# A fixed order of work on five engines, planned with other costs and other due times

## The chip, the cores and the metric

One core of one Trainium2 chip. The metric is the device time of one launch in microseconds, lower is better.

## What is computed

A "macaron" block on x of shape 4 x 2048 x 256, float32: half an MLP, attention, half an MLP, each on a layer-normalised input and added to x.

```
x = x + 0.5 * ffn(layernorm(x))
x = x + attention(layernorm(x))
x = x + 0.5 * ffn(layernorm(x))
```

`ffn` is a gated MLP of width 704, in which the input of each product and each weight is first rounded to a 4-bit grid in blocks of 16 (`scale = max|x|/6`, then the nearest of 0, 0.5, 1, 1.5, 2, 3, 4, 6). `attention` is causal differential attention: 8 heads, each with two score maps of head dimension 16 over queries and keys that are rms-normalised and rotated; the output of a head is `softmax1 @ v - lam * softmax2 @ v`, layer-normalised, then projected.

## The kernel before

The 8192 rows are 64 tiles of 128 rows, and four tiles are a chunk: 16 chunks, 4 to each of the 4 batches. A chunk passes through six kinds of work. (1) First MLP: `stats` and `rstd` (layer norm), then for each pair of tiles `quant_x`, `divide_x`, `square_x`, `grid_x`, `points_x`, `dequant_x`, `high_x`, `low_x` (the 4-bit rounding, split into two float16 halves) and `turn_x`, a transposing DMA; for each tile three `hidden` products (L1311), `tanh` and `gate` for each, the same chain of rounding for the hidden row (`quant_h` ... `turn_h`), the `down` product (L1324), and `add_down`. (2) Projections: `norm_x`, `transpose_x` (L1300), `copy_xT`, `project_qk` and `project_v` (L1332), `read_qk`, `read_v`, `rope`, `rope_add`. (3) `rms` for the chunk, then `norm_qk`, `high_qk`, `low_qk`, `turn_qk` for each tile. (4) Attention of the chunk: for each of 4 groups of two heads and each key tile up to the diagonal one step. A step has two `scores` stages (L1347), two `exp` stages (L1074), a `mask` on the diagonal, and one `values` stage (L1365). A chunk has 16, 32, 48 or 64 steps by its place in its batch, 640 in all. Each group ends in `copy_o`, `transpose_o` (L1372), `heads_out`. (5) `head_stats`, `norm_heads`, `transpose_x`, `project_out` (L1379), `add_out`. (6) Second MLP, as the first, and the store.

PE (tensor) has all products and transposes; DVE (vector) the statistics, scales, gates, the low halves and sums; ACT (scalar) tanh, squares, copies and exp; POOL (gpsimd) four of the rounding steps, `rope_add`, `low_qk`, `mask` and `rstd`; SP issues the DMAs. `rms` (L1214) and `head_stats` (L1270) are one row and then the helper `rsqrt` (L465 to L474), twelve small DVE instructions that wait for one another.

What sets the order: `whole_plan` lists every stage with its engine, its weight (us), a due time, what it needs, which buffers it takes and which it frees. `Plan.order` then places stages one at a time. Among the stages whose needs are met it takes the one that can start first, and of those that can start at once the one with the smallest due time. The result is one list for each engine, and the emission below walks through these lists. So each engine's queue is fixed when the kernel is built, and a stage that waits holds back all behind it on its engine. The rings of buffers (two score buffers, three of probabilities, three shared PSUM banks, the MLP's rows and others) are dealt out in the order in which the plan takes them, and the waits for a free buffer follow from that.

The weights come from `COST`, or from `whole_plan` for `scores`, `exp` and `values`. To those of every engine but PE `START` (0.05) is added, and between engines `LAG` (0.12) passes. The due times come from `DUE`: `lead` and `spans` lay out the chunks on an axis (`spans` by the chunk's place in its batch), the pairs `mlp1`, `qkv`, `qk`, `out`, `mlp2` are an offset and a pace in hundredths of the chunk's span, and `nudge` shifts each kind of stage by a number of its own.

Of the kernel before, what the change touches and what calls it, by code (L numbers as in the profile page):

```python
# [44 lines left out]
NTC = 4  # L45
# [10 lines left out]
DUE = dict(lead=57, spans=(23, 55, 57, 15), tail=50208, early=1.97, mlp1=(85, 27), qkv=(-162, 60), qk=(-77, 71), out=(-188, 149), mlp2=(99, 30),  # L56
           nudge=dict(add_down=-22, add_out=18, copy_o=13, copy_xT=50, dequant_h=-57, dequant_x=-38,
                      divide_h=38, divide_x=5, down=-15, exp=222, gate=-22, grid_h=8, grid_x=-8,
                      head_stats=27, heads_out=29, hidden=-47, high_h=-47, high_qk=-154, high_x=15,
                      load=6, low_h=-29, low_qk=3, low_x=28, mask=-58, norm_heads=-50, norm_qk=-4,  # L60
                      norm_x=-27, points_x=31, project_out=-16, project_qk=-9, quant_h=61,
                      quant_x=57, read_qk=-26, read_v=-15, rms=2, rope=19, rope_add=30, rstd=40,
                      scores=-242, square_h=-29, stats=-37, store=-29, tanh=32, transpose_o=-26,
                      transpose_x=-28, turn_h=6, turn_qk=5, turn_x=-26, values=5))
# [16 lines left out]
COST = dict(add_down=0.46, add_out=0.42, copy_o=0.68, copy_xT=0.38, dequant_h=1.42, dequant_x=1.12,  # L81
            divide_h=1.45, divide_x=1.11, down=2.19, gate=0.82, grid_h=1.72, grid_x=1.33, head_stats=4.21,
            heads_out=3.64, hidden=1.27, high_h=0.79, high_qk=1.14, high_x=0.63, low_h=1.18, low_qk=2.46,
            low_x=1.03, mask=0.69, norm_heads=0.55, norm_qk=0.87, norm_x=0.6, points_h=1.71, points_x=1.29,
            project_out=1.09, project_qk=2.13, project_v=1.0, quant_h=1.83, quant_x=2.78, read_qk=0.6,
            read_v=0.38, rms=7.63, rope=1.93, rope_add=1.38, rstd=2.9, square_h=1.61, square_x=1.29,
            stats=2.3, tanh=0.46, transpose_o=0.58, transpose_x=0.33)
START = 0.05
LAG = 0.12


def attention_steps():


    out, diagonals = [], 0
# [17 lines left out]
class Plan:  # L113
# [12 lines left out]
    def add(self, name, engine, weight, due, needs=(), takes=(), frees=(), lands=0.0):  # L126
        weight = COST.get(name[0], weight)
# [3 lines left out]
    def order(self):  # L131
        end, free_at = {}, dict.fromkeys(ENGINES, 0.0)
# [1281 lines left out]
```

## Time and profile before

| | |
|---|---|
| median of 3 runs | 2468.85 us (2467.5 to 2469.09) |
| the profiled execution | 2471.45 us |
| its span, first to last instruction | 2469.5 us |
| mean granted clock of TensorE | 0.937 |

The rows of the trace are given below, in groups. A busy time is that of an engine's own instructions; waiting at a semaphore is idle. PE is the matrix engine, PEld its weight loads, which overlap it.

### The profile page before, as it was taken

The page shows a single profiled execution, that of the slowest core. Times are in us where ns is not written, and L with a number is a line of the kernel's source. Part 1 is how long each engine was busy: PE and PEld are TensorE (multiplying, and loading weights), DVE is VectorE, ACT ScalarE, POOL GpSimd, SP SyncE. Part 2 cuts the span into 40 slices and gives each one's busy share as a digit, 9 for nine tenths or more (in the row PEclk, how much of TensorE's full clock was granted, in tenths as well). Part 3 has the DMA queues.
Part 4 walks back from the last instruction along what each step waited for, and adds up shares of the span by engine and source line. Part 5 has one row for each costly group of instructions (what it writes and reads, how often), then busy time and mean ns, then how long its engine had stood idle before and what let it go on. Part 6 is the DMA issues. An engine that isn't in the chain of part 4 may idle for free.

```text
span 2469.5 us, 39323 instructions
## 1 busy us (share of the span) xinstructions
PE 2099.7 (85%) x13502; PEld 839.6 (34%) x13502; DVE 1831.3 (74%) x3615; ACT 1777.8 (72%) x2660; POOL 1658.3 (67%) x1520
## 2 busy tenths in 40 slices
PE   1567999899897889899998889989898889998965
PEld 1233433233333333333333333333333333332322
DVE  6888787668758888777858888886867888873434
ACT  2345677978875778778786778877787677887852
POOL 3887666766756687876766677886776677862415
PEclk8788999999998999999998999999999999998986
DMA  3122322221312132232321322223241223221101
GB/s 92 34 40 55 65 49 49 47 53 30 68 39 52 19 63 50 56 66 44 55 58 19 53 48 63 60 33 71 33 84 21 47 32 79 49 50 34 33 1 41
DMA packets 409906, 119.36 MB, mean 48 GB/s; under 512 B 390638, under 2 KB 409454, under 8 KB 409710
## 3 DMA queue, kind: packets, MB, share of 16 engines
q1 hardware_dynamic: 409710, 116.86, 25.1%
q8 instruction: 109, 1.79, 0.3%
q14 instruction: 87, 0.71, 0.1%
HBM read 11.96 MB, written 8.39 MB: 8 GB/s over the span
## 4 chain that ended last, share of the span: by engine, by line
PE 45%; DVE 20%; ACT 8%; POOL 5%; issue 5%; DMA 2%; SPq 1%; ACTq 0%; DVEq 0%; POOLq 0%
PE psum_o L1365 11%; PE shared L1311 10%; PE shared L1324 7%; PE psum_s L1347 7%; ACT probs L1074 6%; PE shared L1332 4%; PE shared L1379 3%; DVE nwt L473 2%; DVE nwt L472 2%; DVE h L1166 1%; PE shared L1300 1%; DMA q_stack<-st_q 1%; DVE nwt L474 1%; POOL grid L965 1%; POOL hq L961 1%
## 5 line engine op out<-in xcount | busy, mean ns | idle before, releaser
L1074 ACT ACTIVATE probs<-psum_s 128x1024 f32<-128x1024 f32 (+3 forms) x1280 | 1092.0, 896 | 234.2 <-PE psum_s L1347 170.9
L1365 PE MATMUL psum_o<-probs,v_sb 128*32 128x512 f32 (+3 forms) x5120 | 590.6, 546 | 9.5 <-POOL probs L995 8.9
L1311 PE MATMUL shared<-w_gu_T,xT 128*128 128x480 f16 (+1 forms) x2304 | 522.6, 371 | 68.5 <-DMA xT<-x 44.4
L1347 PE MATMUL psum_s<-q_stack,k_stack 64*128 64x512 f16 (+3 forms) x2560 | 431.7, 359 | 113.6 <-ACT probs L1074 97.1
L1324 PE MATMUL shared<-w_down_T,hT 128*128 128x256 f16 (+1 forms) x2176 | 315.5, 292 | 77.3 <-DVE hq L1156 55.9
L1347 PEld LDWEIGHTS psum_s<-q_stack,k_stack 64*128 64x128 f16 x2560 | 110.1, 93 | 652.6 <-ACT probs L1074 465.9
L1311 PEld LDWEIGHTS shared<-w_gu_T,xT 128*128 128x128 f16 x2304 | 207.1, 99 | 352.7 <-issue 119.4
L995 POOL TENSOR_SCALAR_AFFINE_SELECT probs<-probs 128x512 f32<-128x512 f32 x256 | 172.6, 679 | 225.7 <-ACT probs L1074 224.4
L961 POOL TENSOR_TENSOR hq<-grid,hq 128x704 f32<-128x704 f32 x128 | 222.7, 1740 | 99.8 <-ACT grid L1019 99.7
L1009 ACT ACTIVATE hq<-shared,tanh_scale 128x240 f32<-128x240 f32 (+1 forms) x384 | 172.6, 454 | 155.7 <-PE shared L1311 143.9
L1324 PEld LDWEIGHTS shared<-w_down_T,hT 128*128 128x128 f16 (+1 forms) x2176 | 204.1, 103 | 193.5 <-issue 76.6
L1154 DVE SCALAR_TENSOR_TENSOR hq<-hq,shared 128x240 f32<-128x240 f32 (+1 forms) x384 | 147.6, 384 | 131.2 <-ACT hq L1009 130.1
L937 POOL TENSOR_TENSOR hq<-hq,rscale 128x704 f32<-128x704 f32 x128 | 186.9, 1463 | 80.0 <-DVE rscale L1100 80.0
L965 POOL TENSOR_TENSOR grid<-hq,grid 128x704 f32<-128x704 f32 x128 | 224.8, 1756 | 8.5
L1166 DVE TENSOR_TENSOR h<-hq,h 128x704 f16<-128x704 f32 x128 | 157.7, 1232 | 63.7 <-ACT h L1027 63.2
L1332 PE MATMUL shared<-w_qkv_T,xT 128*128 128x512 f32 (+1 forms) x512 | 196.9, 517 | 1.3 <-ACT xT L1036 0.8
L969 POOL TENSOR_TENSOR hq<-grid,qscale 128x704 f32<-128x704 f32 x128 | 182.7, 1427 | 8.9
L1365 PEld LDWEIGHTS psum_o<-probs,v_sb 128*32 128x32 f32 x5120 | 110.5, 109 | 186.0 <-issue 145.6
L1156 DVE SCALAR_TENSOR_TENSOR hq<-hq,shared 128x240 f32<-128x240 f32 (+1 forms) x384 | 152.8, 398 | 13.2
L1019 ACT ACTIVATE grid<-grid 128x704 f32<-128x704 f32 (+1 forms) x192 | 141.5, 737 | 6.1
L986 POOL TENSOR_TENSOR st_q<-roped,st_q 128x512 f16<-128x512 f32 x64 | 79.0, 1235 | 90.7 <-ACT st_q L1064 90.6
L1027 ACT ACTIVATE h<-hq 128x704 f16<-128x704 f32 x128 | 100.8, 788 | 42.1 <-POOL hq L969 28.7
(120 smaller groups left out, 2848.2 us busy)
## 6 DMA issues: line engine op xcount, KB each, us to landing
xb<-L_attn_x SPq DMA_DIRECT2D x16, 512.0 KB, 4.0
out<-xb SPq DMA_DIRECT2D x16, 512.0 KB, 3.3
hT<-h SPq DMA_TRANSPOSE x128, 3.5
xT<-x SPq DMA_TRANSPOSE x64, 3.1
k_stack<-st_k SPq DMA_TRANSPOSE x64, 3.3
q_stack<-st_q SPq DMA_TRANSPOSE x64, 3.3
k_stack<-L_ffn_w_down SPq DMA_DIRECT2D x1, 704.0 KB, 8.7
k_stack<-L_ffn_w_gate SPq DMA_DIRECT2D x1, 480.0 KB, 4.6
```

The source lines that it names most:

```text
L937: nc.gpsimd.tensor_tensor(by_block(a), by_block(a), rscale[:, i, 0:nb].unsqueeze(2).broadcast_to([P, nb, QB]), ALU.mult).then_inc(scaled_r ...
L961: nc.gpsimd.tensor_tensor(a, g, a, ALU.add).then_inc(grid_ready, 1)
L965: nc.gpsimd.tensor_tensor(g, a, g, ALU.subtract).then_inc(grid_ready, 1)
L969: nc.gpsimd.tensor_tensor(by_block(a), by_block(g), qscale[:, i, 0:nb].unsqueeze(2).broadcast_to([P, nb, QB]), ALU.mult).then_inc(quantise ...
L995: nc.gpsimd.affine_select(out=blk, in_=blk, compare_op=ALU.is_ge, fill=0.0, base=0, pattern=[[0, 4], [1, P]], channel_multiplier=-1)\
L1074: nc.scalar.activation(probs[:, s % 3, 2 * u:2 * u + 2, q0:CHUNK], psum_s[u][:, :, q0:CHUNK], ACT.Exp, scale=HD ** -0.5 / QK_SCALE ** 2).t ...
L1166: nc.vector.tensor_tensor(low, buffers(kind, key)[0], high, ALU.subtract)\
L1311: last = nc.tensor.matmul(bank(e)[:, 0:2 * (hi - lo)], xs[:, x, t % 2, k, :], w_gu_T[:, w, k, 2 * lo:2 * hi], start=n == 0, stop=n == len( ...
L1324: last = nc.tensor.matmul(bank(e)[:, 0:C], hs[0:n, k, :], w_down_T[0:n, w, :], start=i == 0, stop=i == len(parts) - 1)
L1332: last = nc.tensor.matmul(bank(e)[:, 0:hi - lo], xT[:, XT[1, t] % ROWS, k, :], w_qkv_T[:, k, lo:hi], start=k == 0, stop=k == KC - 1)
L1347: last = nc.tensor.matmul(psum_s[u][:, j, q0:CHUNK], k_stack[half, at, h, kt % NTC * P:(kt % NTC + 1) * P], q_stack[half, c % 2, h, q0:CHU ...
L1365: last = nc.tensor.matmul(psum_o[at:at + VD, q0:CHUNK], v_sb[:, kt // NTC % SLOTS * NTC + kt % NTC, 2 * g + u, :], probs[:, s % 3, 2 * u + ...
```

## The change

Every instruction stays, and the code that emits them is untouched. The plan changes in these points.

- `START` and `LAG` go. A stage now leaves its engine `OVERLAP` earlier than its weight says (0.08 DVE, 0.10 ACT, 0.04 POOL), while its result is ready only at the full weight, on PE 0.14 later (`DRAIN`). A stage of another engine meets it after `REACH` (0.04 to 0.14 by the engine that waits), a freed buffer after `RELEASE` (0.06).
- PE's tiling is followed: `scores` and `values` each have one of their own and all else a third. A PE stage whose tiling is another than the last one's starts `SWITCH` (0.11) later, and the choice of the next stage sees that.
- The costs are new; those of `rms` and `head_stats` rise, those of `project_qk`, `project_v` and `values` fall.
- `norm_x` of a chunk from the fourth on needs the last `norm_heads` of the chunk three before.
- `DUE` is wholly new.

```diff
--- before.py
+++ after.py
@@ -53,15 +53,15 @@
 
 
 
-DUE = dict(lead=57, spans=(23, 55, 57, 15), tail=50208, early=1.97, mlp1=(85, 27), qkv=(-162, 60), qk=(-77, 71), out=(-188, 149), mlp2=(99, 30),
-           nudge=dict(add_down=-22, add_out=18, copy_o=13, copy_xT=50, dequant_h=-57, dequant_x=-38,
-                      divide_h=38, divide_x=5, down=-15, exp=222, gate=-22, grid_h=8, grid_x=-8,
-                      head_stats=27, heads_out=29, hidden=-47, high_h=-47, high_qk=-154, high_x=15,
-                      load=6, low_h=-29, low_qk=3, low_x=28, mask=-58, norm_heads=-50, norm_qk=-4,
-                      norm_x=-27, points_x=31, project_out=-16, project_qk=-9, quant_h=61,
-                      quant_x=57, read_qk=-26, read_v=-15, rms=2, rope=19, rope_add=30, rstd=40,
-                      scores=-242, square_h=-29, stats=-37, store=-29, tanh=32, transpose_o=-26,
-                      transpose_x=-28, turn_h=6, turn_qk=5, turn_x=-26, values=5))
+DUE = dict(lead=6900543696, spans=(22, 77, 47, 13564), tail=3021347, early=0.16, mlp1=(9, 17), qkv=(-59, 98), qk=(-183, 113), out=(-142, 85), mlp2=(207, 79),
+           nudge=dict(add_out=-7, copy_o=-67, copy_xT=-18, dequant_h=5, dequant_x=-1, divide_x=-28,
+                      down=15, exp=-12, gate=43, grid_h=6, grid_x=4, head_stats=102, heads_out=-15,
+                      hidden=89, high_h=-4, high_qk=211, high_x=-3, load=11, low_h=4, low_qk=-30,
+                      low_x=79, mask=14, norm_qk=-4, norm_x=-8, points_h=-131, points_x=-11,
+                      project_out=-20, project_qk=10, project_v=120, quant_h=-5, quant_x=-17,
+                      read_qk=54, read_v=34, rms=30, rope=110, rope_add=63, rstd=57, scores=-167,
+                      square_h=-5, square_x=28, stats=101, store=-7, tanh=-107, transpose_o=-7,
+                      transpose_x=-11, turn_h=20, turn_qk=-6, values=34))
 ST = 2
 LANDING = 4.0
 XU = 2
@@ -78,15 +78,19 @@
 HALF = P // 2
 
 KTILES = [(lo + i * (hi - lo) // 2, (hi - lo) // 2) for lo, hi in PARTS for i in range(2)]
-COST = dict(add_down=0.46, add_out=0.42, copy_o=0.68, copy_xT=0.38, dequant_h=1.42, dequant_x=1.12,
-            divide_h=1.45, divide_x=1.11, down=2.19, gate=0.82, grid_h=1.72, grid_x=1.33, head_stats=4.21,
-            heads_out=3.64, hidden=1.27, high_h=0.79, high_qk=1.14, high_x=0.63, low_h=1.18, low_qk=2.46,
-            low_x=1.03, mask=0.69, norm_heads=0.55, norm_qk=0.87, norm_x=0.6, points_h=1.71, points_x=1.29,
-            project_out=1.09, project_qk=2.13, project_v=1.0, quant_h=1.83, quant_x=2.78, read_qk=0.6,
-            read_v=0.38, rms=7.63, rope=1.93, rope_add=1.38, rstd=2.9, square_h=1.61, square_x=1.29,
-            stats=2.3, tanh=0.46, transpose_o=0.58, transpose_x=0.33)
-START = 0.05
-LAG = 0.12
+COST = dict(add_down=0.47, add_out=0.42, copy_o=0.68, copy_xT=0.38, dequant_h=1.43, dequant_x=1.1,
+            divide_h=1.46, divide_x=1.1, down=2.07, gate=0.82, grid_h=1.74, grid_x=1.37, head_stats=6.25,
+            heads_out=3.38, hidden=1.23, high_h=0.79, high_qk=1.14, high_x=0.63, low_h=1.23, low_qk=2.48,
+            low_x=0.96, mask=0.68, norm_heads=0.45, norm_qk=0.88, norm_x=0.82, points_h=1.76, points_x=1.37,
+            project_out=0.87, project_qk=1.75, project_v=0.87, quant_h=2.05, quant_x=2.87, read_qk=0.59,
+            read_v=0.37, rms=9.04, rope=1.93, rope_add=1.32, rstd=2.7, square_h=1.61, square_x=1.29,
+            stats=1.81, tanh=0.45, transpose_o=0.56, transpose_x=0.28)
+OVERLAP = dict(tensor=0.0, vector=0.08, scalar=0.1, gpsimd=0.04, sync=0.0)
+REACH = dict(tensor=0.14, vector=0.04, scalar=0.04, gpsimd=0.08, sync=0.1)
+RELEASE = 0.06
+DRAIN = 0.14
+TILING = dict(scores=1, values=2)
+SWITCH = 0.11
 
 
 def attention_steps():
@@ -125,7 +129,9 @@
 
     def add(self, name, engine, weight, due, needs=(), takes=(), frees=(), lands=0.0):
         weight = COST.get(name[0], weight)
-        self.stages[name] = (engine, weight + START * (engine != "tensor"), due + self.nudge.get(name[0], 0),
+        if engine == "tensor":
+            lands += DRAIN
+        self.stages[name] = (engine, weight, due + self.nudge.get(name[0], 0),
                              [n for n in needs if n], list(takes), list(frees), lands)
 
     def order(self):
@@ -134,6 +140,7 @@
         self.ring = {r: {} for r in self.sizes}
         banks = [[0.0, 0] for _ in range(BANKS)]
         out = {e: [] for e in ENGINES}
+        tiling, left = 0, {}
         missing = {name: len(stage[3]) for name, stage in self.stages.items()}
         needed_by = {name: [] for name in self.stages}
         for name, stage in self.stages.items():
@@ -169,6 +176,8 @@
                 at = ready(name)
                 if at is not None:
                     start = max(at, free_at[self.stages[name][0]])
+                    if self.stages[name][0] == "tensor" and TILING.get(name[0], 0) != tiling:
+                        start += SWITCH
                     if best is None or (round(start, 6), place[name]) < best[:2]:
                         best = (round(start, 6), place[name], start, name)
             assert best, "stages that wait for one another: " + str(list(met)[:20])
@@ -182,18 +191,20 @@
                     banks[b] = [math.inf, banks[b][1] + 1]
                 else:
                     self.ring[r].setdefault(user, len(self.ring[r]))
-            free_at[engine] = start + weight
+            free_at[engine] = left[name] = start + weight - OVERLAP[engine]
+            if engine == "tensor":
+                tiling = TILING.get(name[0], 0)
             end[name] = start + weight + lands
             for n in needed_by[name]:
                 missing[n] -= 1
                 if not missing[n]:
-                    met[n] = max(end[m] + (LAG if self.stages[m][0] != self.stages[n][0] else 0)
-                                 for m in self.stages[n][3])
+                    met[n] = max(end[m] + REACH[self.stages[n][0]] if self.stages[m][0] != self.stages[n][0] else
+                                 left[m] for m in self.stages[n][3])
             for r, user in frees:
                 if r == "bank":
-                    banks[self.bank[user][0]][0] = end[name] + LAG
+                    banks[self.bank[user][0]][0] = end[name] + REACH["tensor"]
                 else:
-                    freed[r][self.ring[r][user]] = end[name] + LAG
+                    freed[r][self.ring[r][user]] = end[name] + RELEASE
             out[engine].append(name)
         self.length = max(end.values())
         self.end = end
@@ -301,7 +312,8 @@
         roots(("stats", 1, c), s0 + (due["qkv"][0] - 2) * k, [("add_down", 0, t) for t in tiles])
         for i, t in enumerate(tiles):
             d = s0 + (due["qkv"][0] + due["qkv"][1] * i) * k
-            add(("norm_x", 1, t), "vector", .5, d, [("rstd", 1, c)], [("xrow", (1, t))],
+            add(("norm_x", 1, t), "vector", .5, d,
+                [("rstd", 1, c), ("norm_heads", NTC * (c - 2) - 1) if c >= 3 else None], [("xrow", (1, t))],
                 [("stats", (1, c))] if i == NTC - 1 else [])
             transposed(1, t, d + .5, [("norm_x", 1, t)])
             before = lambda name: (name, t - 1) if t else None
@@ -334,15 +346,15 @@
             w = (CHUNK - q0) / CHUNK
             for u in range(2):
                 before = s - 1 + u, 1 - u
-                add(("scores", s, u), "tensor", .24 * w, d + u * .1,
+                add(("scores", s, u), "tensor", .22 * w, d + u * .1,
                     [("turn_qk", tiles[-1]), ("scores", s - 1, 1) if s else None],
                     [("scores", (s, u))])
-                add(("exp", s, u), "scalar", .12 + .85 * w, d + u * .1,
+                add(("exp", s, u), "scalar", .17 + .855 * w, d + u * .1,
                     [("scores", s, u), ("exp", *before) if s or u else None], [("probs", s)], [("scores", (s, u))])
             if diag is not None:
                 add(("mask", s), "gpsimd", .62, d + .3, [("exp", s, 1)])
             d += (CHUNK - q0) * k
-            add(("values", s), "tensor", .94 * w, d, [("mask", s) if diag is not None else ("exp", s, 1),
+            add(("values", s), "tensor", .87 * w, d, [("mask", s) if diag is not None else ("exp", s, 1),
                                                       ("values", s - 1) if s else None, ("read_v", tiles[-1])],
                 [("psum_o", (c, g))], [("probs", s)])
             if is_last:
```

## Rows read from the trace of the kernel before

**Rows 1.** The page's span and busy time of each engine
```profile
span 2469.5 us, 39323 instructions
...
PE 2099.7 (85%) x13502; PEld 839.6 (34%) x13502; DVE 1831.3 (74%) x3615; ACT 1777.8 (72%) x2660; POOL 1658.3 (67%) x1520
```

**Rows 2.** Windows, whole core; columns us, busy us, granted clock, DMA share, GB/s
```profile
0.00:80.00 80.00, 14.53 (x71) 11.75 (x72) 54.19 (x118) 21.79 (x44) 36.62 (x49) 0.80 0.30 77
80.00:300.00 220.00, 164.88 (x920) 77.45 (x918) 183.32 (x336) 116.74 (x202) 171.72 (x140) 0.85 0.29 52
300.00:2200.00 1900.00, 1721.57 (x11239) 680.84 (x11241) 1483.64 (x2934) 1469.81 (x2193) 1347.88 (x1241) 0.96 0.26 49
2200.00:2390.00 190.00, 158.93 (x1117) 48.62 (x1115) 74.74 (x161) 149.95 (x190) 64.93 (x62) 0.94 0.15 30
2390.00:2469.50 79.50, 39.79 (x164) 20.91 (x164) 35.39 (x72) 19.55 (x34) 37.18 (x30) 0.67 0.15 32
```

**Rows 3.** Windows of 100 us, the same columns
```profile
700.00:800.00 100.00, 85.71 (x558) 34.54 (x555) 75.89 (x155) 68.90 (x110) 59.99 (x63) 0.91 0.19 36
...
1300.00:1400.00 100.00, 84.16 (x588) 36.55 (x584) 81.11 (x162) 66.77 (x110) 59.68 (x60) 0.93 0.22 36
...
1900.00:2000.00 100.00, 83.73 (x569) 35.24 (x568) 83.36 (x183) 67.91 (x108) 61.61 (x73) 0.91 0.22 38
2100.00:2200.00 100.00, 97.32 (x633) 39.76 (x635) 79.72 (x154) 80.80 (x121) 79.61 (x67) 1.00 0.23 46
```

**Rows 4.** Waits of PE, 300 to 2200; us in total, times, longest us
```profile
PE psum_s L1347 <- ACT probs L1074: 79.1, 161, 1.6
PE shared L1324 <- DVE hq L1156: 31.2, 9, 5.3
PE shared L1300 <- DVE hq L1156: 19.1, 4, 6.8
PE shared L1300 <- DVE xb L1173: 9.1, 4, 2.4
...
PE shared L1300 <- DVE xrow L1277: 5.7, 4, 2.3
PE shared L1311 <- DVE hq L1156: 5.4, 3, 4.9
```

**Rows 5.** Groups of instructions, busy us, mean ns, idle before: rms and head_stats
```profile
L473 DVE TENSOR_TENSOR nwt<-nwt 128x32 f32<-128x32 f32 (+1 forms) x96 | 51.3, 535 | 3.3
L472 DVE TENSOR_TENSOR nwt<-nwt 128x32 f32<-128x32 f32 (+1 forms) x96 | 50.1, 522 | 3.3
...
L474 DVE SCALAR_TENSOR_TENSOR nwt<-nwt 128x128 f32<-128x128 f32 (+1 forms) x64 | 37.4, 584 | 2.2
...
L465 DVE TENSOR_SCALAR nwt<-nwt 128x128 f32<-128x128 f32 (+1 forms) x32 | 25.1, 785 | 1.1
...
L466 DVE TENSOR_SCALAR nwt<-nwt 128x128 uint32<-128x128 uint32 (+1 forms) x32 | 19.7, 617 | 0.0
L468 DVE TENSOR_SCALAR nwt<-nwt 128x128 int32<-128x128 int32 (+1 forms) x32 | 18.9, 591 | 1.1
...
L1270 DVE TENSOR_SCALAR nwt<-head_ssq 128x32 f32<-128x32 f32 x16 | 11.9, 746 | 0.4
...
L1214 DVE TENSOR_SCALAR nwt<-qk_ssq 128x128 f32<-128x128 f32 x16 | 11.2, 698 | 0.4
```

**Rows 6.** Source line L466; ns min/median/max, first and last start us
```profile
L466 DVE TENSOR_SCALAR nwt<-nwt x32: 168/217/1724, 174.6 to 2387.1; 128x128 uint32<-128x128 uint32 x16, 128x32 uint32<-128x32 uint32 x16
```

**Rows 7.** Timeline of ACT from 807, of PE from 704; start us, us
```profile
807.61 7.56 ACT L1074 ACTIVATE probs<-psum_s 128x1024 f32<-128x1024 f32 x8
...
704.32 0.60 PE L1347 MATMUL psum_s<-q_stack,k_stack 64*128 64x512 f16 x4
704.86 1.06 PE L1365 MATMUL psum_o<-probs,v_sb 128*32 128x512 f32 x8
705.89 0.39 PE L1347 MATMUL psum_s<-q_stack,k_stack 64*128 64x512 f16 x2
```

## The prediction

> **What bounds the kernel now.** I read the page's first part first: TensorE is busy 2099.7 of 2469.5 us, the other three engines 67 to 74% [rows 1]. PE's own work is the largest sum. As the change keeps every instruction, time can come only from the 370 us in which PE stands still, or from the clock at which it works. The profiled execution took 2471.45 us, 1.95 around its span; that is 2.6 above the median of the runs, 2468.85. The sum below is made against 2471.45.
>
> The stretches say where PE stands still [rows 2]. The first 80 us prepare the weights (65 us idle, nothing of it planned by this code). From 80 to 300 the first chunks fill the machine (55 idle). From 300 to 2200 all passes run beside one another: 1721.57 of 1900 busy, 178.4 idle, mean granted clock 0.96. From 2200 to 2390 the last attention chunk runs with little beside it (31 idle), and the last 79.5 us are the last chunk's output and second MLP, with nothing left beside them (40 idle). The long middle is where an order can matter. Its hundreds of microseconds are not alike [rows 3]: 2100 to 2200 has 97.3 us of PE at full clock, while 700, 1300 and 1900 have 84 to 86 at 0.91 to 0.93. These three lie where one batch ends and the next begins with its short causal chunks.
>
> Who ended PE's waits in the middle [rows 4]: exp freeing a score buffer, 79.1 us in 161 short waits of 0.5 us; and long waits at the head of the queue, the `down` products and the transposes L1300 behind DVE work, 31.2 us in 9 waits (3.5 each) and 19.1 in 4 (4.8 each), with 20.2 in 11 more on the next three rows. The first kind belongs to the two-deep score ring. The second is what a wrong plan looks like: PE's fixed list puts an item next whose input or bank is several microseconds late, and all the attention queued behind it stands too. DVE rows end 70.5 us of these.
>
> **The change part by part.** No instruction is added or removed, in compute or in DMA; each engine's list, SP's included, is permuted, and buffers are dealt again to users. So the price of a part is only what it does to waits.
>
> *DVE costs and overlap.* The list of DVE must be in step with the others. Two stages, `rms` and `head_stats`, are a scalar row and the inverse-root helper, 16 calls each. Their eight main rows add up to 25.1+19.7+18.9+50.1+51.3+37.4+11.9+11.2 = 225.6 us, 7.05 us per call [rows 5]. The old plan held them for (7.63+4.21)/2+0.05 = 5.97, the new one for (9.04+6.25)/2-0.08 = 7.57. So the old lists were 1.08 us late at each of 32 calls, 35 us in all; the middle is 1900 of the 2212 us in which these calls occur [rows 6], so 30 us of it. DVE is busy 78% there [rows 2], and I let its free 22% absorb that share: 23 us reaches PE, as part of the 70.5 us above. The bounds are 0 and 70.5 less, and on the other side nothing excludes a loss: the boundary windows bound it, below. I take 23 because it is the one lateness that rows measure.
>
> *ACT and PE costs.* Eight full exps back to back take 7.56 us, 0.945 each [rows 7]; the old plan says 1.02, the new one 0.925. On PE two full scores stages take 0.54 (704.32 to 704.86) and the values stage up to the next scores 1.03 (704.86 to 705.89) [rows 7]. The old plan has 2 x 0.24 and 0.94, no switch; the new one 2 x 0.22+0.11 and 0.87+0.11. So the old plan saw an attention step as 2.04 of ACT against 1.42 of PE, where the rows give 1.89 against 1.57 and the new plan 1.85 against 1.53. It believed that there was 0.6 us of room for MLP work per step, and there was 0.3. Correcting that can thin out the 79.1 us of exp waits, or add to them, if more exps are set in a row with nothing between. Ends: 79 less; or, if the middle waited at the last attention stretch's rate (31 of 190 idle against 178 of 1900), (31/190-178.4/1900) x 1900 = 132 more. I take 0, since the ring's depth stays and these waits are short.
>
> *`norm_x` needs the `norm_heads` of three chunks before* (c from 3, 13 chunks, 52 stages). Both are DVE's, so no wait is emitted, only the order is tied. Projection runs ahead of output by design; cost 0, unless it is what holds a batch's first projections back (rival 3).
>
> *Reach, release, drain.* A uniform 0.12 becomes 0.04 to 0.14 by engine, 0.14 after PE. These decide near-ties among items that start within a tenth of a microsecond. 0 of itself; ends included in the two above.
>
> *The new due times* set which of several ready stages goes first. Head and tail: from 80 to 300 and after 2390 the chain of dependencies has few alternatives; I take 0 for both, with ends of 20 less (under half of the 55 idle) and 15 more.
>
> *Clock.* In the middle the granted clock is 0.96, the mix of the two levels 2.4 and 1.2 GHz, so 1900 x 0.04 = 76 us of full clock are missing. The windows where PE is best filled have 1.00, the worst 0.91 [rows 3]. If waits shrink by 23 of 178, a like part of 76 is 10 us; half of it, 5, since part of the slow time is PE waiting anyway. Ends 0 and 20.
>
> Sum: 2471.45 - 23 - 5 = 2443.
>
> **The rivals.** *1. Much faster.* All of the misplaced items go, and the middle runs at 95% of PE, between its mean 90.6 and its best window. 1721.57/0.95 = 1812, 88 less: 2383. For it: such windows exist in this very trace [rows 3]. Against: two thirds of the 178 us then have to go, with the exp waits left in place.
>
> *2. No change.* A fixed list can hold only a mean, and the real durations are not near theirs. L466, one small DVE operation, takes 168 ns at least, 217 at the median and 1724 at most [rows 6], mean 617 [rows 5]. So (617-217)/617 = 65% of its time is standing. If the eight rows stand alike, 0.65 x 225.6 = 146 us is standing; a fifth more, 29 us, in an order that packs DVE and POOL closer gives all 28 us back: 2470. POOL, the engine that a closer packing sets beside it, is busy 71% of the middle [rows 2].
> The Trainium skill (GPSIMD Engine Reference, Specifications and Key points) says that GpSimd shares its SBUF interfaces with VectorE and contends with DVE instructions that use two ports or have two SBUF inputs. This would be the cause of that spread, and speaks against a plan that gains by closer packing; the trace shows the spread in L466 but names no cause. By that rule the sum is this rival's, by the mean costs alone it is the forecast's.
>
> *3. Slower: the batch boundary.* The due positions of the projections are parts of the chunk's own span, and the new spans are 22, 77, 47 and 13564. For the first chunk of batches 2 to 4 the span is the long one. With qkv=(-59, 98) its four tiles are due at -59, 39, 137 and 235% of it; its scores, from 100% on. So where several are ready, tiles 2 and 3 lose against the batch's other work, although no score of that chunk can start before all four are turned. In the old plan, (-162, 60) puts all four before 18%. Attention would then be missing at the three boundaries, where PE is already weak: 14.3+15.8+16.3 = 46.4 us idle in three windows [rows 3]. Doubling that: 2471.45 + 46.4 - 28 = 2490. It decides from the point at which the boundaries lose more than 28 us, 9 each. Against: a ready projection on an idle PE is taken whatever its due time, since the earliest start goes first, and norm and transposes precede it by needs alone.
>
> **How the numbers follow.** About 0.2% is what a measurement of this kernel can tell from no change, some 5 us. Forecast 0.56, rival 1 0.11, rival 2 0.13, rival 3 0.20. Faster 0.67, same 0.13, slower 0.20. The forecast's own range, with the clock, head and a part of the exp term, is 2410 to 2463. The whole range reaches to rival 1 (2385) and into rival 3 as far as 2482, with about 0.08 left out below and 0.11 above.
>
> **What would show it.** Right: instruction counts alike; in the middle PE's long waits behind DVE (L1324, L1300, L1311) fall from 70 us to under 50, their longest from 5 to 7 us to 3 or 4; PE busy about alike or slightly smaller, clock above 0.96; the middle about 28 us shorter, head and tail within 10. Exp waits near 79 us. The two DVE stages near 7 us per call. Wrong: waits behind DVE alike or larger; exp waits over 110; a dip below 80 at each batch boundary with scores waiting for the q_stack transfer (rival 3); the mean of L466 and its kin up by a fifth and DVE's busy sum up by 25 us or more (rival 2); or a gain that lies in the first 300 or last 270 us.

## The result, and the profile of the changed kernel

The changed kernel takes 2477.45 us (median of 20 runs, 2467.07 to 2484.6), the kernel before 2469.28 on the same chips: ratio 1.0031, 95% interval 1.0022 to 1.004. It is slower by 0.31%, some 8 us. The forecast was 2443. The rows below are from an execution of 2476.07 us. Lines 465 to 474 of before are 477 to 486 now, as all later lines 12 higher.

The page of the changed kernel, span and busy time of each engine:

```profile
span 2474.1 us, 39316 instructions
...
PE 2060.2 (83%) x13502; PEld 844.6 (34%) x13502; DVE 1854.0 (75%) x3615; ACT 1773.8 (72%) x2660; POOL 1670.0 (67%) x1520
```

Against [rows 1] the counts are the same, PE is busy 39.5 us less, DVE 22.7 us more. So PE does the same work in less time, and stands idle 413.9 us where it was 369.8, 44.1 more. That is the whole riddle: the change gave PE 39.5 us and took 44.1 away. The granted clock, 0.942 against 0.937, is the higher of the two and has no part in the loss.

Its windows, in the columns of [rows 2]; the first three are the hundreds of microseconds in which batches meet, the last four whole stretches:

```profile
700.00:800.00 100.00, 85.11 (x579) 34.50 (x583) 75.27 (x154) 73.24 (x113) 63.39 (x65) 0.91 0.21 38
1300.00:1400.00 100.00, 84.12 (x591) 37.97 (x589) 88.21 (x177) 68.75 (x114) 66.68 (x68) 0.91 0.22 39
1900.00:2000.00 100.00, 86.24 (x608) 37.12 (x604) 90.78 (x192) 70.85 (x115) 65.20 (x74) 0.91 0.23 38
...
80.00:300.00 220.00, 160.43 (x865) 80.80 (x864) 194.54 (x337) 112.33 (x200) 185.35 (x148) 0.88 0.29 53
300.00:2200.00 1900.00, 1685.58 (x11223) 680.61 (x11222) 1495.99 (x2927) 1462.61 (x2182) 1344.56 (x1230) 0.96 0.26 49
2200.00:2390.00 190.00, 160.72 (x1187) 50.32 (x1185) 70.72 (x149) 158.02 (x203) 66.90 (x65) 0.98 0.17 32
2390.00:2474.10 84.10, 39.58 (x164) 21.07 (x164) 39.60 (x89) 19.66 (x34) 37.21 (x30) 0.66 0.14 30
```

The boundary windows are as weak as before and no weaker [rows 3], and the middle does about the same number of products in 1900 us (11223 against 11239) with 36 us less of PE's busy time [rows 2].

Waits of PE from 300 to 2200 us in the changed kernel; us in total, times, longest us:

```profile
PE psum_s L1359 <- ACT probs L1086: 113.5, 224, 1.7
PE psum_o L1377 <- DVE o_sb L1245: 15.4, 11, 2.6
PE shared L1336 <- DVE hq L1168: 10.3, 6, 2.1
PE shared L1323 <- DVE hq L1168: 10.1, 11, 1.9
PE shared L1312 <- DVE hq L1168: 9.8, 11, 2.4
...
PE shared L1312 <- DVE xrow L1289: 7.1, 8, 1.6
PE shared L1323 <- DVE xb L1185: 4.3, 6, 1.2
```

The long waits that I had read as the plan's error are gone. Those of L1336, L1312 and L1323 behind DVE add up to 47.4 us in eight rows (five of them above, three small) and the longest is 2.4 us, not 6.8. In [rows 4] they were 70.5, and 72.2 with one small row that it leaves out. But other waits have come behind DVE: all of them together are 71.0 us, 74.6 before, in 73 short ones instead of 31. Over the whole span they are 131.8 us, 130.7 before. And exp now ends 113.5 us of PE's waits, 34.4 more than in [rows 4].

Groups of instructions of the changed kernel; busy us, mean ns, idle before:

```profile
L485 DVE TENSOR_TENSOR nwt<-nwt 128x32 f32<-128x32 f32 (+1 forms) x96 | 48.5, 505 | 3.3
...
L478 DVE TENSOR_SCALAR nwt<-nwt 128x128 uint32<-128x128 uint32 (+1 forms) x32 | 20.7, 647 | 0.0
...
L1145 DVE TENSOR_SCALAR xq<-xb,mean_var,rstd 128x256 f32<-128x256 f32 x128 | 116.5, 950 | 14.3 <-POOL rstd L969 14.0
...
L1178 DVE TENSOR_TENSOR h<-hq,h 128x704 f16<-128x704 f32 x128 | 173.4, 1355 | 54.7 <-ACT h L1039 54.5
...
L1289 DVE TENSOR_TENSOR xrow<-heads,head_rstd 128x256 f32<-128x256 f32 x64 | 40.3, 666 | 9.0 <-PE shared L1312 8.5
```

The same three groups in the trace of before, which stand in no row ahead of the prediction:

```profile
L1166 DVE TENSOR_TENSOR h<-hq,h 128x704 f16<-128x704 f32 x128 | 157.7, 1232 | 63.7 <-ACT h L1027 63.2
L1133 DVE TENSOR_SCALAR xq<-xb,mean_var,rstd 128x256 f32<-128x256 f32 x128 | 83.6, 694 | 9.2 <-POOL rstd L957 9.0
L1277 DVE TENSOR_TENSOR xrow<-heads,head_rstd 128x256 f32<-128x256 f32 x64 | 27.0, 453 | 6.8 <-PE shared L1300 6.2
```

This is where the plan's picture breaks. The same instructions on the same data have other durations in another order. The two stages of [rows 5] fell from 225.6 to 194.2 us (their eight rows, 6.07 us a call; the new plan holds 7.57 for them), while L1145 rose by 32.9, L1178 by 15.7 and L1289 by 13.3. The new costs of `rms` (9.04), `head_stats` (6.25) and `quant_x` (2.87) are their mean durations in the old trace, from first to last instruction. They describe the order that the plan has just thrown away.

### The profile page after: what moved, and what is told of

The parts are those of the page before. It is cut to its first block, busy times and chain, and to the rows that moved or that the text cites. A ratio compares the mean times of both kernels' runs of the same rounds, so it can differ in the third digit from the quotient of the medians.

```text
span 2474.1 us, 39316 instructions
## 1 busy us (share of the span) xinstructions
PE 2060.2 (83%) x13502; PEld 844.6 (34%) x13502; DVE 1854.0 (75%) x3615; ACT 1773.8 (72%) x2660; POOL 1670.0 (67%) x1520
## 4 chain that ended last, share of the span: by engine, by line
PE 31%; DVE 29%; ACT 12%; POOL 10%; issue 7%; DMA 3%; SPq 1%; ACTq 0%; DVEq 0%; POOLq 0%
PE psum_o L1377 9%; ACT probs L1086 9%; PE shared L1336 5%; PE shared L1323 5%; PE psum_s L1359 4%; PE shared L1344 4%; DVE amax L1109 3%; DVE xq L1145 2%; DVE h L1178 2%; POOL grid L977 2%; PE shared L1391 2%; DVE hq L1168 2%; DVE qscale L1111 2%; POOL hq L973 2%; POOL hq L949 2%
## 5 line engine op out<-in xcount | busy, mean ns | idle before, releaser
L1086 ACT ACTIVATE probs<-psum_s 128x1024 f32<-128x1024 f32 (+3 forms) x1280 | 1067.9, 898 | 180.7 <-PE psum_s L1359 154.5
L1377 PE MATMUL psum_o<-probs,v_sb 128*32 128x512 f32 (+3 forms) x5120 | 608.4, 566 | 37.1 <-DVE o_sb L1245 16.2
L1323 PE MATMUL shared<-w_gu_T,xT 128*128 128x480 f16 (+1 forms) x2304 | 495.1, 366 | 65.9 <-DMA xT<-x 44.5
L1359 PE MATMUL psum_s<-q_stack,k_stack 64*128 64x512 f16 (+3 forms) x2560 | 407.2, 360 | 149.0 <-ACT probs L1086 136.0
L1336 PE MATMUL shared<-w_down_T,hT 128*128 128x256 f16 (+1 forms) x2176 | 302.2, 284 | 58.5 <-DVE hq L1168 41.1
L1323 PEld LDWEIGHTS shared<-w_gu_T,xT 128*128 128x128 f16 x2304 | 218.0, 99 | 326.8 <-issue 62.4
L1359 PEld LDWEIGHTS psum_s<-q_stack,k_stack 64*128 64x128 f16 x2560 | 98.9, 94 | 588.4 <-ACT probs L1086 497.8
L1336 PEld LDWEIGHTS shared<-w_down_T,hT 128*128 128x128 f16 (+1 forms) x2176 | 201.2, 100 | 176.6 <-issue 77.0
L1166 DVE SCALAR_TENSOR_TENSOR hq<-hq,shared 128x240 f32<-128x240 f32 (+1 forms) x384 | 147.8, 385 | 103.5 <-ACT hq L1021 102.8
L1178 DVE TENSOR_TENSOR h<-hq,h 128x704 f16<-128x704 f32 x128 | 173.4, 1355 | 54.7 <-ACT h L1039 54.5
L1377 PEld LDWEIGHTS psum_o<-probs,v_sb 128*32 128x32 f32 x5120 | 116.3, 111 | 272.3 <-issue 193.6
L1344 PE MATMUL shared<-w_qkv_T,xT 128*128 128x256 f32 (+1 forms) x512 | 191.8, 509 | 16.2 <-DVE hq L1168 10.5
L1029 ACT ACTIVATE grid<-hq 128x704 f32<-128x704 f32 x128 | 101.5, 793 | 49.9 <-POOL hq L949 49.8
```

Source lines behind the costliest of these rows:

```text
L1086: nc.scalar.activation(probs[:, s % 3, 2 * u:2 * u + 2, q0:CHUNK], psum_s[u][:, :, q0:CHUNK], ACT.Exp, scale=HD ** -0.5 / QK_SCALE ** 2).t ...
L1178: nc.vector.tensor_tensor(low, buffers(kind, key)[0], high, ALU.subtract)\
L1323: last = nc.tensor.matmul(bank(e)[:, 0:2 * (hi - lo)], xs[:, x, t % 2, k, :], w_gu_T[:, w, k, 2 * lo:2 * hi], start=n == 0, stop=n == len( ...
L1336: last = nc.tensor.matmul(bank(e)[:, 0:C], hs[0:n, k, :], w_down_T[0:n, w, :], start=i == 0, stop=i == len(parts) - 1)
L1344: last = nc.tensor.matmul(bank(e)[:, 0:hi - lo], xT[:, XT[1, t] % ROWS, k, :], w_qkv_T[:, k, lo:hi], start=k == 0, stop=k == KC - 1)
L1359: last = nc.tensor.matmul(psum_s[u][:, j, q0:CHUNK], k_stack[half, at, h, kt % NTC * P:(kt % NTC + 1) * P], q_stack[half, c % 2, h, q0:CHU ...
```

## The experiments

**What makes a duration depend on the order.** The timelines of DVE and of POOL in the kernel before, side by side in the same microseconds, suggest it; start us, us:

```profile
808.48 0.42 DVE L1259 TENSOR_REDUCE head_ssq<-o_norm 128x8 f32<-128x256 f32 x1
808.93 1.52 DVE L1270 TENSOR_SCALAR nwt<-head_ssq 128x32 f32<-128x32 f32 x1
810.49 0.18 DVE L465 TENSOR_SCALAR nwt<-nwt 128x32 f32<-128x32 f32 x1
810.58 1.67 DVE L466 TENSOR_SCALAR nwt<-nwt 128x32 uint32<-128x32 uint32 x1
812.28 0.18 DVE L468 TENSOR_SCALAR nwt<-nwt 128x32 int32<-128x32 int32 x1
812.50 1.26 DVE L472 TENSOR_TENSOR nwt<-nwt 128x32 f32<-128x32 f32 x1
```

```profile
808.74 1.68 POOL L961 TENSOR_TENSOR hq<-grid,hq 128x704 f32<-128x704 f32 x1
810.49 1.72 POOL L965 TENSOR_TENSOR grid<-hq,grid 128x704 f32<-128x704 f32 x1
812.29 1.42 POOL L969 TENSOR_TENSOR hq<-grid,qscale 128x704 f32<-128x704 f32 x1
```

L1270, an instruction like L465 of 0.18 us below it, begins at 808.93 inside POOL's L961 and is done when that is (810.45 against 810.42). L465 then slips into the gap, L466 stands until L965 ends (812.25, 812.21), L468 slips into the next gap, L472 stands until L969 ends. The standing engine's time is booked as its own busy time. Over the whole trace it is always one class of DVE instruction that stands: TENSOR_SCALAR from SBUF to SBUF, and those with two tensor inputs in SBUF. All 470 DVE instructions of before that last over 1.5 times the shortest of their line and shape are of this class, and so are all 522 of after. It goes the other way round too: the GpSimd L961 that begins at 1104.80, 0.35 us after a DVE L1166, takes 2.33 us, where its median is 1.68.

*Theory A (exclusion).* These DVE instructions and GpSimd's exclude each other, each side waiting for the other's whole instruction; the plan gives both engines mean costs and so counts the standing as if it were a fixed price. *Rival B (mean costs).* The mean costs are good enough, and the loss is something else in the plan: its due times, or its ring of score buffers.

To put numbers on A, I walked the fixed lists of a kernel through its own dependencies with either the mean costs of the new table or the bare durations and the exclusion. For before and after this gives 2318.4 and 2283.3 by mean costs, so the new plan promised 35 us; with the exclusion 2364.0 and 2386.7, 23 us slower. These are replays of lists, not times of a chip, and leave out the clock and what lies around the plan. A third replay has the bare durations and no exclusion; it gives 2244.3 and 2234.5.

**e4_side_block** measures the exclusion by itself: two blocks behind the kernel of after, DVE's the same in both, with 20 GpSimd adds beside the first only.

```diff
+        for busy in (True, False):
+            with nc.Block() as block:
+                if busy:
+                    @block.gpsimd
...
+                            nc.gpsimd.tensor_tensor(grid[:, i % 2, :], hq[:, 0, :], hq[:, 1, :], ALU.add)
...
+                @block.vector
...
+                        # 8 each: reduce; tensor_scalar; tensor_tensor SBUF+SBUF; tensor_tensor SBUF+PSUM
```

> The changed kernel with two blocks behind it that compute nothing of use: VectorE runs 8 reduces of 256 columns (one SBUF source), 8 tensor_scalar (SBUF to SBUF), 8 tensor_tensor with two SBUF sources and 8 with one source in PSUM, first while GpSimd runs 704-column tensor_tensor without a break, then with GpSimd idle. Theory A (the instruction that uses the second SBUF port and any GpSimd instruction exclude one another whole): in the first block the tensor_scalar and the two-SBUF-source tensor_tensor wait for the end of a GpSimd instruction, so that they take up to 1.7 us and some 1.5 us at the median, GpSimd's get longer in turn by 0.2 to 0.4; the reduces and those with a PSUM source take what they take alone. Theory B (a general slowing by shared bandwidth): all four kinds get longer by some tens of per cent, none by a factor. In the second block all take their bare 0.2 to 0.5 us.

DVE's timeline in the two blocks, first with GpSimd at work (GpSimd's 20 took 34.38 us from 2475.82), then without; start us, us:

```profile
2477.48 1.06 DVE L1412 TENSOR_REDUCE qscale<-probs 128x8 f32<-128x256 f32 x3
2478.46 12.52 DVE L1416 TENSOR_SCALAR probs<-probs 128x256 f32<-128x256 f32 x8
2490.90 14.52 DVE L1419 TENSOR_TENSOR probs<-probs 128x256 f32<-128x256 f32 x8
2505.35 2.73 DVE L1422 TENSOR_TENSOR roped<-probs,psum_o 128x256 f32<-128x256 f32 x8
...
2512.20 1.06 DVE L1412 TENSOR_REDUCE qscale<-probs 128x8 f32<-128x256 f32 x3
2513.18 1.70 DVE L1416 TENSOR_SCALAR probs<-probs 128x256 f32<-128x256 f32 x8
2514.79 2.76 DVE L1419 TENSOR_TENSOR probs<-probs 128x256 f32<-128x256 f32 x8
2517.47 2.73 DVE L1422 TENSOR_TENSOR roped<-probs,psum_o 128x256 f32<-128x256 f32 x8
```

Eight TENSOR_SCALAR take 12.52 us instead of 1.70, eight TENSOR_TENSOR from SBUF 14.52 instead of 2.76: about one per GpSimd add of 1.72 us. The reduces and those with one input in PSUM are untouched. A is shown as a mechanism. The Trainium skill (Advanced Engine Details and Errata, VectorE Performance Modes) says that GpSimd and two-port Vector instructions "will interfere/block eachother"; the rows agree (12.52 us instead of 1.70), and say that it is a wait for a whole instruction.

**e8_before_no_port and e9_after_no_port** take the exclusion away from each order. GpSimd's elementwise work is replaced by pow on a few columns, of like duration, which doesn't make DVE stand. The rounding steps, `rope_add`, `low_qk` and `mask` are thereby left out; all waits and lists stay.

```diff
-                            nc.gpsimd.tensor_tensor(a, g, a, ALU.add).then_inc(grid_ready, 1)
+                            k = 5 if e[1] == "x" else 7
+                            nc.gpsimd.tensor_tensor(a[:, 0:k], spin_in[:, 0:k], spin_by[:, 0:k], ALU.pow).then_inc(grid_ready, 1)
```

> The kernel before, order and all, in which GpSimd's elementwise work on the data is left out: in the place of each such instruction it raises two to seven columns of constants to a power, as its own root step in rstd does (1.04 us for four columns, and VectorE's instructions beside that step did not wait for it). GpSimd should stay as busy as it was, within 5%, without using the port. If the exclusion is what VectorE loses, VectorE's busy sum falls by 350 to 420 us from 1831, and replaying the lists with bare durations and no exclusion gives 120 us less, so 2350, down to 2330 if the clock gains with it. If VectorE's long instructions have another cause, nothing changes but the durations of GpSimd.

> The same done to the changed kernel. Replaying its lists without exclusion gives 152 us less than with it, and 10 less than those of before. So if the exclusion is what took the gain back, this is faster than e8_before_no_port by 5 to 20 us, where the changed kernel is 8 us slower than before. If it is something else in the order (exp waits, a tighter order that breaks at any disturbance, the batch boundary), it stays slower than e8 by 8 us or more.

They took 2327.54 us (ratio to before 0.9425, 0.9405 to 0.9445) and 2326.86 (0.9423, 0.9408 to 0.9438). The page of e8, one of its groups of instructions and PE's waits for exp over the whole span, then the same of e9:

```profile
span 2326.5 us, 39327 instructions
...
PE 2058.2 (88%) x13502; PEld 828.0 (36%) x13502; DVE 1460.9 (63%) x3615; ACT 1770.1 (76%) x2660; POOL 1494.5 (64%) x1524
```

```profile
L475 DVE TENSOR_TENSOR nwt<-nwt 128x32 f32<-128x32 f32 (+1 forms) x96 | 23.4, 244 | 3.3
```

```profile
PE psum_s L1349 <- ACT probs L1076: 93.3, 198, 2.2
```

```profile
span 2323.8 us, 39320 instructions
...
PE 2017.8 (87%) x13502; PEld 841.5 (36%) x13502; DVE 1458.2 (63%) x3615; ACT 1762.4 (76%) x2660; POOL 1483.2 (64%) x1524
```

```profile
L487 DVE TENSOR_TENSOR nwt<-nwt 128x32 f32<-128x32 f32 (+1 forms) x96 | 23.4, 244 | 3.3
```

```profile
PE psum_s L1361 <- ACT probs L1088: 140.3, 274, 1.7
```

Three things follow. The row that was 535 ns in [rows 5] and 505 in after is 244 in both: the order no longer changes this duration once the exclusion is gone. DVE's busy time falls by 370 us from [rows 1], PE's waits behind DVE in the middle from 74.6 us to 8.2 (in e9 8.1), and the kernel by 142. (POOL is busy 10% less, where I wanted at most 5, so a part of the 142 is lighter work.) And after's deficit against before, 8.2 us, becomes 0.7 us of advantage, which is within the noise of four runs each, while the 8.2 isn't. So the exclusion carries the deficit, with the reserve that the lighter GpSimd work can have a part in it. But it carries no more: about 9 of the 36 us between forecast and result. The new order ought then to have won, and doesn't. PE is busy 40.4 us less in e9 than in e8, and its waits for exp over the whole span are 140.3 us against 93.3, 47.0 more. The trade of PE time against exp waits is there without the exclusion.

**e1_new_costs_old_due** keeps the new planner and costs, with the due times of before.

```diff
-DUE = dict(lead=6900543696, spans=(22, 77, 47, 13564), tail=3021347, early=0.16, ...
+DUE = dict(lead=57, spans=(23, 55, 57, 15), tail=50208, early=1.97, ...
```

> The changed planner (costs, overlap, reach, drain, switch, the need of norm_x) with the due times of before. It tells which half of the change moves the time. If the planner's better costs help by themselves (the prediction's reasoning), this is faster than before, 2445 to 2465. If an order is good only together with the due times that were fitted to its exact costs, this is slower than before and than the changed kernel: replaying its lists stage by stage with the new plan's costs gives 26 us more than the lists of before (2344.7 against 2318.4), and replaying them with VectorE's and GpSimd's instructions excluding one another gives 34 more, so 2480 to 2504. PE's changes between tilings fall from 2053 to 1462 in either case, and PE's busy sum by 30 to 60 us.

It took 2535.35 (1.0267, 1.025 to 1.0284), above what was expected. Its page, and the first of its waits of PE from 300 to 2200:

```profile
span 2531.4 us, 39323 instructions
...
PE 2080.7 (82%) x13502; PEld 855.6 (34%) x13502; DVE 1785.2 (71%) x3615; ACT 1779.9 (70%) x2660; POOL 1663.7 (66%) x1520
```

```profile
PE psum_s L1359 <- ACT probs L1086: 129.8, 186, 4.4
```

A better table of costs with due times fitted to another one costs 66 us. The due times are no free-standing knob: they are fitted to the planner's numbers. Of the two halves of the change, the new planner and costs alone lose 66 us and the refit takes 58 back. (The other half alone doesn't exist: with the new due times the old planner finds no order in which its stages don't wait for one another. The new need of `norm_x` leaves every list as it is when taken out: cost 0, as forecast.)

**e5, e6, e10, e12: a planner that knows the exclusion.** Each DVE and GpSimd stage is placed instruction by instruction, with bare durations, and an instruction of the class waits for the other engine's.

```diff
+            took, exclusive, gap = inside[i]
+            if exclusive:
+                t = max(t, lock["gpsimd" if engine == "vector" else "vector"])
+                lock[engine] = t + took - HOLD
```

e5 has the due times of before; e6, e10 and e12 have due times searched under this planner, in two searches that both start from those of before (e6, e10), the first of them carried on for longer (e12). **e7 and e11** are the control: the change's own planner, with due times from the same kind of search under mean costs, twice.

> The changed planner in which the stages of VectorE and GpSimd are laid out instruction by instruction with their bare durations, and those of VectorE that use the second SBUF port exclude GpSimd's (each holds the other off until 0.135 us before its end). The due times are those of before, nothing is searched. Two theories give numbers that lie far apart. Mean costs (what the change believes): its lists take 2434 in the plan's own units, where those of before take 2318, so 116 us slower than before, about 2585. Exclusion: 2351 against 2364 for the lists of before, 13 faster, so 2456 to 2475 with what the clock adds or takes.

> The same planner with exclusion, and due times searched for it (22800 tries from those of before). Mean costs: its lists take 2374 against 2318 for before, 56 us slower, about 2525. Exclusion: 2267 against 2364, 97 faster; the clock gave back up to two thirds of a difference between before and the changed kernel, so 2372 to 2440.

> Control: the changed kernel's planner, untouched, with other due times, found by as long a search (22700 tries from those of before) that knows mean costs alone. Mean costs: 2278 against 2318 for before and 2283 for the changed kernel, so 40 faster than before, about 2430. Exclusion: 2341 against 2364 for before and 2387 for the changed kernel, so 23 faster than before and 45 faster than the changed kernel, 2440 to 2465. If the changed kernel is only one draw of many that look alike to its planner, this one lands elsewhere although the planner rates the two within 6 us.

> A second, independent search with exclusion in the plan (22600 tries from the due times of before). Mean costs: its lists take 2380 against 2318 for before, 62 us slower, about 2530. Exclusion: 2273.5 against 2364, and 7 more than the first such order, which took 2389.5 on the chip: 2385 to 2420. If the first one's gain was a lucky draw, this one lies anywhere between 2440 and 2530.

> A second, independent search with the changed kernel's own planner (22500 tries, a worse end). Mean costs: its lists take 2303.7 against 2318 for before, 15 us faster, about 2455. Exclusion: 2383 against 2364, so 19 slower, almost where the changed kernel stands (2387): 2470 to 2490. As in the changed kernel the two theories differ in sign here.

> The first order with exclusion, searched on (48900 more tries): its plan takes 2258.6 in place of 2266.5. If the plan's gains are still real at this size, 2380 to 2388; if the search has begun to fit the plan's own errors, no faster than 2389.5.

All orders, the two replays of their lists, and what was measured (us; the interval is that of the ratio to before):

```
order                      by mean costs  by exclusion  measured  ratio to before
before                         2318.4        2364.0      2469.28
after (the change)             2283.3        2386.7      2477.45  1.0022 to 1.004
e1  new costs, old due         2344.7        2398.4      2535.35  1.025  to 1.0284
e5  exclusion, old due         2434.1        2350.9      2530.3   1.0221 to 1.0266
e6  exclusion, own due         2374.0        2266.5      2389.5   0.9657 to 0.9706
e7  mean costs, other due      2277.9        2341.2      2456.21  0.9935 to 0.9968
e10 exclusion, second          2380.0        2273.5      2415.79  0.9759 to 0.9798
e11 mean costs, second         2303.7        2383.3      2526.42  1.0208 to 1.0248
e12 exclusion, longer          2367.4        2258.6      2426.86  0.981  to 0.985
```

By mean costs the nine orders have no relation to the chip (correlation -0.08). By the exclusion it is 0.86; the best three on the chip are the best three there, and each costs more by mean costs than after does. e6 was expected at 2525 by the mean costs and took 2389.5. It beats both kernels, by 3.2% and 3.5%, with the same instructions. The control tells this from the mere length of a search: e7 and e11, searched as long but by mean costs, are at 2456 and 2526.

The control says something of the change itself as well. Its planner rates e7, after and e11 within 26 us of one another, all below before; on the chip they are 12 below, 8 above and 57 above it. So the change's 8 us are one draw of a planner whose orders of like promise lie 70 us apart. The exclusion has the sign of all three (23 below, 23 above, 19 above).

One rival isn't excluded by these orders: that it is the bare durations, laid out instruction by instruction, which help, and not the exclusion. No order was planned with the one and without the other. The third replay, bare durations alone, correlates at 0.79 over the nine; over the six orders that weren't searched under the exclusion it has 0.84, the exclusion 0.47 and the mean costs 0.65. It has e5 right, 56 us behind before, where the exclusion puts it 13 ahead. But it puts after 10 us ahead of before and e6 only 13, where the chip has 8 behind and 79 ahead and the exclusion 23 behind and 97 ahead.

The page of e6 and its first two waits of PE from 300 to 2200:

```profile
span 2395.6 us, 39320 instructions
...
PE 2037.2 (85%) x13502; PEld 848.3 (35%) x13502; DVE 1804.7 (75%) x3615; ACT 1776.4 (74%) x2660; POOL 1671.9 (70%) x1520
```

```profile
PE psum_s L1394 <- ACT probs L1121: 112.9, 187, 2.5
PE psum_o L1412 <- POOL probs L1042: 9.5, 13, 2.2
```

Its exp waits are those of after (112.9, 113.5), its DVE busy sum is 49.3 us smaller and PE's 23.0, and the waits behind DVE in the middle add up to 32.4 us instead of 71.0 (e10 29.8, e12 53.1; the control e7 57.0, e11 75.3). The DVE sum alone doesn't set the time: e1's is 1785.2, smaller still, in the slowest order of all.

The misses count too. e5's list is 13 us shorter than before's by the exclusion and was 61 us slower on the chip. e12's search found 7.9 us more than e6 by its own measure, and the chip was 37.4 slower. e1 ended 31 us above the higher end expected, e5 and e11 55 and 36 us above the exclusion's ranges. Measured less exclusion replay lies between 91 and 179 us. An order that a search picks is also one that flatters the model's errors. What makes up that spread (the clock, 0.928 in e1 and 0.953 in e6, is one part and also a consequence) stays open. So the exclusion explains the direction of the change and much of the differences between orders; it doesn't predict 10 us, and e5 shows that it misses some 70.

## Why the prediction was wrong

*DVE's lateness, 23 us less.* This is the step that failed. Its reading of PE's wait rows was right: the long waits behind DVE were the plan's error, and they went, 72.2 to 47.4 us, 24.8 less, about the size forecast. What failed is the silent sentence behind it, that lateness taken off one place isn't made at another. The gain was paid out in L1377's new wait for `o_sb` (15.4 us) and small ones, so that all waits behind DVE fell by 3.6 in the middle and rose by 1.1 over the span. That these waits come from the exclusion is shown: without it 8 us of them are left in either order. Why they moved is argued: 9.04 and 6.25 aren't costs but averages over one pairing with GpSimd, and a plan that takes them for costs is late or early in the next pairing. In the new pairing `rms` is 7.63, and those of `quant_x` are 3.38 instead of 2.87, 64 stages, 33 us. The lateness itself was under-read: the eight rows leave out 32 of L474 and the gaps between instructions, and whole stages took (9.04+6.25)/2 = 7.65 us, so the old lists were 1.68 late at a call, not 1.08.

*Exp waits, 0.* This step failed as well. They rose by 34.4 us in the middle (38.9 over the span, 97.1 to 136.0), inside the ends of -79 and +132. e9 against e8 shows the same rise with the exclusion gone, so it belongs to the new order itself. All eight orders of the new planner, whatever their due times, wait longer for exp over the span (111.7 to 187.2 us) than before's does. Why is argued, not shown: the new plan gives a step 1.53 of PE beside 1.85 of ACT, so it sees less room between exps than before for MLP work, and it packs like stages together to save tiling changes. With two score buffers a longer run of other work on PE would then be a wait.

*PE's tiling, reach and drain, 0.* Under-read. The new lists change the tiling 1429 times, the old 2053. PE's busy time fell by 39.5 us for 624 changes fewer, 0.06 each, and by 40.4 from e8 to e9 for the same 624. The starts of consecutive stages of like size give 0.09 (scores) and 0.12 (values) more where the tiling changes, near `SWITCH` 0.11. Some of the 39.5 is the clock: from before to e8, with the same lists, PE's busy time fell by 41.5 us as the granted clock rose from 0.937 to 0.964, and at that rate the 0.005 from before to after is 8 us (an estimate). A term that I left at nothing because it decides near-ties only was the change's real gain. The Trainium skill (TensorEngine Tiling (Array Packing), Key Properties) says that a change of tiling mode drains TensorE; that the rows show a price at each change agrees with it.

*Clock, 5 us less.* 0.942 against 0.937, 0.96 in the middle in both: the sign was right, and the waits that it should have rewarded hadn't shrunk.

*Head, tail, `norm_x`.* At 2390 us both kernels have 164 products left. The last stretch is 84.1 us against 79.5, with 89 DVE instructions in it and not 72 [rows 2]: 4.6 us, within the 15 allowed, and as much as the whole span's difference. It was put at 0.

*The sum.* Over the whole span: -39.5 of PE's work, +38.9 of exp waits, +1.1 of waits behind DVE, and 4.1 in what I haven't followed one by one: +4.6 in span. So the loss is a small remainder of two large terms that I had put at 0; the rows of PE's waits don't say where in it the exclusion's 9 us lie. That it came out near no change is luck of that balance.

*The rivals.* Rival 2 named the mechanism, a fixed list that holds only means, and priced it: it would give all 28 us back. That was right in kind and 7 us too kind in size. Its own test, L466's mean up by a fifth, failed (617 to 647 ns); the standing went to other rows, and DVE's busy sum rose by 22.7, near its 25. The rule of the Trainium skill that it cited spoke against the change, and I gave it 0.13. Rival 3 isn't what happened, though the sign was its: the boundary windows are unchanged. Rival 1 needed exp waits to stay in place while all else went; e6 comes near its 2383 us, by another planner.

## What to carry to other kernels

Where the durations of one instruction spread by a factor of ten (168 to 1724 ns in [rows 6]), its mean isn't a cost, and a plan fitted to means can move the loss rather than remove it, as it did here. Ask first what the long ones end together with. Measure the bare duration, put the cause of the spread into the planner as a resource, and refit the due times in the same step; new costs under old due times lost 66 us here.

A busy sum that falls on the bound engine is worth nothing unless its waits stay put: read the idle time by releaser beside it, and price the waits that closer grouping makes.

## What I had not expected of the hardware

- One GpSimd instruction holds back a whole DVE TENSOR_SCALAR (SBUF to SBUF) or TENSOR_TENSOR (two SBUF inputs) for as long as it runs: 1.56 us instead of 0.21 for one of 256 columns. It goes the other way round too, up to 2.33 us for a GpSimd instruction of 1.68. The time counts as busy. In this kernel the removal of it is worth up to 142 of 2469 us.
- Reduces and instructions with one input in PSUM run beside GpSimd unhindered (2.73 us for eight in both blocks), and GpSimd's pow on a few columns doesn't hold DVE back (244 ns in e8, where POOL is busy 64%).
- A change of PE's tiling costs about 0.1 us from start to start (0.09 and 0.12), and with 624 fewer PE's busy time was 39.5 us less (40.4 between e8 and e9).
